# Softmax row sums written to PSUM, one eviction moved from VectorE to ScalarE, three PSUM banks for the rest, and new instruction orders in a fused adaLN block

## The reference

```
mod = silu(c) @ wmod            -> sa, ca, ga, sb, cb, gb per batch
h   = layernorm(x) * (1 + ca) + sa
q, k, v = (h @ W + b).reshape(b, 16 heads, 8, 256)
attn = softmax(einsum('bhdt,bhds->bhts', k, v) * temperature, axis=-1)
x   = x + ga * einsum('bhdt,bhts->bhds', q, attn)
h   = layernorm(x) * (1 + cb) + sb
gate, up = fp4_linear(h, w_gate), fp4_linear(h, w_up)      # 352 wide
x   = x + gb * fp4_linear(silu(gate) * up, w_down)
```

## Time and profile before

| what | value |
|---|---|
| median of three runs | 613.52 us (611.83 to 613.89) |
| the profiled execution's own time | 614.23 us |
| its span, first to last instruction | 611.3 us |
| busy: ACT, DVE, PE, POOL | 555.9, 568.7, 558.3, 507.3 us |
| mean granted TensorE clock | 0.962 |
| one batch in the steady stretch | 17.18 us |

### The profile page before, as it was taken

One profiled execution on the slowest core, in us unless ns is written; L12 is line 12 of the kernel. 1 busy time (PEld: TensorE's weight loads), 2 busy tenths in 40 slices (PEclk: granted clock), 3 DMA queues, 4 the chain that ended last, 5 costly groups with the idle time before them and its releaser, 6 DMA issues.

```text
span 611.3 us, 15522 instructions
## 1 busy us (share of the span) xinstructions
PE 558.3 (91%) x4336; PEld 385.6 (63%) x4336; DVE 568.7 (93%) x1124; ACT 555.9 (91%) x2281; POOL 507.3 (83%) x710
## 2 busy tenths in 40 slices
PE   4588999999999999999999999999999999998874
PEld 2465556666666666666666666666666666666653
DVE  5568799999999999999999999999999999999986
ACT  2499899999999999999999999999999999999621
POOL 5544478999999999999999999999999999988741
PEclk9669899999999999999999999999999999999878
DMA  5655556546655556555655556655655556652000
GB/s 156 179 142 143 129 152 163 145 133 170 170 140 147 149 155 173 159 157 137 172 144 143 149 155 171 171 145 139 170 144 141 152 153 174 164 143 58 10 10 26
DMA packets 87888, 86.12 MB, mean 141 GB/s; under 512 B 8566, under 2 KB 83548, under 8 KB 87804
## 3 DMA queue, kind: packets, MB, share of 16 engines
q1 hardware_dynamic: 85372, 83.10, 50.4%
q10 hardware_dynamic: 2432, 2.03, 1.2%
HBM read 47.29 MB, written 37.81 MB: 139 GB/s over the span
## 4 chain that ended last, share of the span: by engine, by line
ACT 52%; PE 18%; issue 13%; DVE 12%; POOL 3%; ACTq 1%; DVEq 0%; POOLq 0%
ACT probs L825 47%; DVE neg_max L1005 6%; PE score_ps L1502 6%; PE bank L1581 5%; PE bank L1570 3%; ACT hT L835 2%; DVE silu_g L1123 2%; ACT hid_T L859 2%; PE bank L1548 2%; PE bank L1606 1%; ACT q_T L841 1%; DVE h_mag L975 1%; POOL hid_q L367 1%; PE bank L1520 1%; DVE h_mag L979 1%
## 5 line engine op out<-in xcount | busy, mean ns | idle before, releaser
L825 ACT ACTIVATE probs<-score_ps,neg_max 128x256 f32<-128x256 f32 x1024 | 483.5, 552 | 5.4 <-DVE neg_max L1005 4.3
L1005 DVE TENSOR_REDUCE neg_max<-score_ps 128x4 f32<-128x1024 f32 x256 | 312.1, 1219 | 19.5 <-PE score_ps L1502 16.8
L825 ACT ACTIVATION_READ_ACCUMULATOR probs<-score_ps,neg_max 128x1 f32 x1024 | 292.4, 286 | 0.0
L1502 PE MATMUL score_ps<-v_stack,k_stack 128*128 128x256 f32 x1024 | 234.9, 333 | 24.2 <-ACT probs L825 21.7
L1502 PEld LDWEIGHTS score_ps<-v_stack,k_stack 128*128 128x128 f32 x1024 | 156.0, 194 | 108.2 <-ACT probs L825 85.1
L1548 PE MATMUL bank<-probs,q_z 128*32 128x256 f32 x2048 | 132.6, 389 | 0.0
L1548 PEld LDWEIGHTS bank<-probs,q_z 128*32 128x32 f32 x2048 | 57.6, 111 | 42.4 <-issue 3.2
L1606 PEld LDWEIGHTS bank<-wd_T,hid_T 118*128 118x128 f32 x384 | 52.7, 201 | 7.6 <-ACT hid_T L859 1.3
L1606 PE MATMUL bank<-wd_T,hid_T 118*128 118x128 f32 x384 | 56.0, 286 | 0.5 <-ACT hid_T L859 0.5
L1570 PE MATMUL bank<-wgu_T,h_T 128*128 128x352 f32 x128 | 52.0, 488 | 1.7 <-ACT h_T L848 0.5
L367 POOL TENSOR_TENSOR hid_q<-hid_r,hid_sc 128x704 f32<-128x704 bf16 x31 | 43.0, 1387 | 7.6 <-DVE hid_r L362 7.5
(11 more groups left out here) (119 smaller groups left out, 880.9 us busy)
## 6 DMA issues: line engine op xcount, KB each, us to landing
split_dram<-kv_hi SPq DMA_DIRECT2D x124, 128.0 KB, 2.6
split_dram<-kv_lo SPq DMA_DIRECT2D x124, 128.0 KB, 2.6
k_stack<-split_dram SPq DMA_DIRECT2D x124, 128.0 KB, 4.5
v_stack<-split_dram SPq DMA_DIRECT2D x31, 512.0 KB, 4.2
mod_bc<-mod_dram SPq DMA_DIRECT2D x32, 256.0 KB, 4.0
x_in<-in_L_attn_x_dram SPq DMA_DIRECT2D x32, 128.0 KB, 3.1
out_dram<-out_t SPq DMA_DIRECT2D x32, 128.0 KB, 3.6
split_dram<-kv_hi ACTq DMA_DIRECT2D x4, 128.0 KB, 2.4
```

The source lines that it names most:

```text
L825: nc.scalar.activation(probs[p][:, h, a, :], score_ps[:, j % 4, a, :], ACT.Exp, bias=neg_max[:, p, n:n + 1], accum_out=row_sum[:, p, h, a: ...
L1005: nc.vector.tensor_reduce(neg_max[:, p, 4 * u:4 * u + 4], score_ps[:, lo:lo + 2, :, :].rearrange("p b a n -> p (b a) n"), AX.X, ALU.max, n ...
L1502: done = nc.tensor.matmul(score_ps[:, j % 4, a, :], k_stack[p][:, h, 128 * a:128 * a + 128], v_stack[p][:, h // R, :], start=True, stop=True)
```

## The change

The row sums of the exponentials go to a PSUM tensor, `row_ps`, which takes `bank_3`. Once per batch ACT copies them to SBUF (`row_sums_out`, 32 columns), in four quarters for the last batch, and DVE's reciprocal waits for that copy. All other PSUM users share `bank_0` to `bank_2`. The high part of v is made on ACT instead of DVE, and DVE's `k_hi` waits for it, since both read the same bank. The bias matmul of q is gone: q's bias is loaded as a column `b_q` and applied by ACT's eviction. POOL's `normalise2` and `scale2` wait for DVE's exponent and magic number of hid of the batch two back. The orders of all five engines are new; SP stores all four parts of a batch one step later in its own numbering and then loads the stacks.

```diff
-TAIL = 39
+TAIL = 37
-        b_raw = sb("b_raw", [64, 3 * D])
-        b_pad = sb("b_pad", [128, 3 * D], F32R)
-        ones_r = sb("ones_r", [128, T], F32R)
+        b_raw = sb("b_raw", [64, 2 * D])
+        b_q = sb("b_q", [128, 1])
+        b_pad = sb("b_pad", [128, 2 * D], F32R)
+        ones_r = sb("ones_r", [128, 128], F32R)
-        bank_xT, bank_kv, bank_q, bank_h2T, bank_mix, bank_down = bank_1, bank_1, bank_2, bank_0, bank_2, bank_3
-        bank_gate, bank_up, bank_hidT = (bank_2, bank_3), (bank_1, bank_0), (bank_2, bank_0)
-        bank_ffw = (bank_0, bank_3, bank_0)
+        bank_xT, bank_kv, bank_q, bank_h2T, bank_mix, bank_down = bank_0, bank_0, bank_1, bank_2, bank_0, bank_1
+        bank_gate, bank_up, bank_hidT = (bank_2, bank_2), (bank_0, bank_1), (bank_1, bank_2)
+        bank_ffw = (bank_2, bank_2, bank_2)
+        row_ps = bank_3[:, 0:2 * H * 2].rearrange("p (b h a) -> p b h a", b=2, a=2)
...
             def normalise2(b, c):
+                if 2 <= b < NB - 4:
+                    pool.wait_ge(hid_z_made, b - 1)
                 normalise2_on(pool, nc.gpsimd, b, c)
             def scale2(b, c):
+                if 2 <= b < NB - 4:
+                    pool.wait_ge(hid_mag_made, b - 1)
                 scale2_on(pool, nc.gpsimd, b, c)
...
-                                         accum_out=row_sum[:, p, h, a:a + 1]).then_inc(exped, 1)
+                                         accum_out=row_ps[:, p, h, a:a + 1]).then_inc(exped, 1)
+            def row_sums_out(b, c):
+                if b == NB - 1:
+                    return
+                act.wait_ge(exped, 2 * H * (b + 1))
+                wait_batches(act, inv_made, b - 1)
+                nc.scalar.activation(row_sum[:, c % 2, :, :], row_ps[:, c % 2, :, :], ACT.Copy).then_inc(row_sums_made, 1)
+            def row_sums_out_part(b, c, r):
+                act.wait_ge(exped, 2 * H * b + 2 * G * (r + 1))
+                wait_batches(act, inv_made, b - 1)
+                nc.scalar.activation(row_sum[:, c % 2, r:H:R, :], row_ps[:, c % 2, r:H:R, :], ACT.Copy)\
+                    .then_inc(row_part[r], 1)
...
+            def v_hi(b, c):
+                wait_batches(act, kv_ps_made, b + 1)
+                wait_dma(act, split_stored, b - 2, STORES * 16)
+                nc.scalar.activation(halves(kv_hi[c % 2][:, 1, :]), kv_rows(1), ACT.Copy).then_inc(v_hi_made, 1)
             def q_out(b, c):
...
-                nc.scalar.activation(q_T[:, c, :, :], halves(bank_q[:, 0:T]), ACT.Copy).then_inc(qT_made, 1)
+                nc.scalar.activation(q_T[:, c, :, :], halves(bank_q[:, 0:T]), ACT.Identity, bias=b_q[:, 0:1])\
+                    .then_inc(qT_made, 1)
...
             def k_hi(b, c):
-                wait_batches(dve, kv_ps_made, b + 1)
+                wait_batches(dve, v_hi_made, b + 1)
...
-            def v_hi(b, c):
-                wait_batches(dve, kv_ps_made, b + 1)
-                wait_dma(dve, split_stored, b - 2, STORES * 16)
-                nc.vector.tensor_copy(halves(kv_hi[c % 2][:, 1, :]), kv_rows(1)).then_inc(v_hi_made, 1)
...
             def row_sums_inv(b, c):
-                wait_batches(dve, exped, b + 1, 2 * H)
+                wait_batches(dve, row_sums_made, b + 1)
...
-                nc.tensor.matmul(bank_q[:, 0:T], w_q[:, :], hT[:, :], start=True, stop=False)
-                nc.tensor.matmul(bank_q[:, 0:T], b_pad[:, 0:D], ones_r[:, :], start=False, stop=True)\
-                    .then_inc(qT_ps_made, 1)
+                nc.tensor.matmul(bank_q[:, 0:T], w_q[:, :], hT[:, :], start=True, stop=True).then_inc(qT_ps_made, 1)
```

More of the change, by code:

```diff
@@ L913, in _ @@
+            last(row_sums_out_part, 31, 2)
+            last(row_sums_out_part, 31, 3)
+            last(tanh, 29, 1)
             last(hidT_out, 28, 0)
@@ L1265, in step @@
             def step(k):
[L1266 to L1279 removed]
+                at(k, 12, silu, 1)
@@ new lines, in _ @@
+            last(hid_exponent, 25)
+            last(k_hi, 30)
+            last(hid_magic, 25)
+            last(maxes, 28, 7)
+            last(v_lo, 30)
+            last(gate2, 24)
+            last(k_lo, 30)
+            last(maxes, 29, 0)
+            last(silu, 26, 0)
+            last(row_sums_inv, 28)
+            last(maxes, 29, 1)
+            last(times_up, 26, 0)
+            last(maxes, 29, 2)
+            last(silu, 26, 1)
+            last(h2_max, 27)
+            last(maxes, 29, 3)
@@ new lines, in _ @@
+            last(hid_magic, 26)
+            last(gate2, 25)
+            last(k_lo, 31)
+            last(maxes, 30, 0)
+            last(silu, 27, 0)
+            last(row_sums_inv, 29)
+            last(maxes, 30, 1)
+            last(times_up, 27, 0)
+            last(maxes, 30, 2)
+            last(silu, 27, 1)
+            last(h2_max, 28)
+            last(times_up, 27, 1)
+            last(maxes, 30, 3)
+            last(h2_recip, 28)
+            last(maxes, 30, 4)
+            last(h2_exponent, 28)
@@ L1417, in _ @@
             last(hid_exponent, 30)
+            last(residual2, 28)
             last(hid_magic, 30)
+            last(silu, 31, 0)
             last(gate2, 29)
-            last(silu, 31, 0)
+            last(hid_sub, 30)
             last(times_up, 31, 0)
-            last(hid_sub, 30)
             last(silu, 31, 1)
```

798 lines of the change are left out of this document (485 added, 313 removed).

## The result

The changed kernel takes **615.97 us** (median of 11 runs, 615.61 to 618.36) against 611.81 (11 runs, 610.01 to 613.89) for the kernel before on the same chip: ratio 1.0078, 95% interval 1.0061 to 1.0094. It is 0.8% slower, where 599 us was forecast. Its profiled span is 616.3 us against 611.3.

The account below looks back on a forecast made before the run. ACT was taken as the fullest engine, DVE next; after the change DVE would set a batch of 16.65 instead of 17.18 us. 614.2 - 15.9 over 30 batches + 0.5 for the tail gave 599 us, range 590 to 623.

Parts of the forecast that it names:

- the sum: Steady batch: DVE, fullest at 16.61 us, sets 16.65, 0.53 less than 17.18; over 30 batches 15.9 us gained.
- The read's slot: ACT's 32 accumulator reads a batch, now to PSUM: each slot 0.03 us shorter than 0.09, 0.96 us a batch.
- ACT in slots: ACT's work per batch counted from start to next start: 16.79 us before, 17.24 with additions, 16.28 after the reads' saving.
- The first rival: ACT's accumulator read slot does not shrink, so ACT sets the batch: slower, 624 us; 24 in 100.
- 0.39 of 17.18 in which ACT waits unseen: ACT in a batch of the kernel before: 16.79 us of slots leave 0.39 us of hidden waiting.
- the hole of 289.46 to 289.85: ACT before an exponential: slot 0.74 instead of 0.45 us, most of the unseen wait; silu and a maximum on DVE precede.
- Orders and banks: Rewritten orders and three PSUM banks instead of four, at PE: counted at nothing, at worst 0.3 us a batch.
- second and third rivals: Second: partial gain, 607 us, 17 in 100. Third: nothing to be seen, 612 to 615 us, 7 in 100.
- The third: Rival: POOL's wait or the three banks eat all the gain, 612 to 615 us; 7 in 100.
- POOL's new wait: POOL waits for DVE's exponent and magic number: counted at nothing, perhaps 0.3 us a batch if its cover is gone.
- The tail: Last term, at the end: last batch's row sums come through ACT copies, adding 0.5 us (0 to 3).
- The head: Start of the kernel, reordered: counted at 0, within 2 us either way.

Follow-up runs that it names:

- x_sbuf: The changed kernel with the row sums written to SBUF as before, without ScalarE's copies; 3% over the changed kernel, 0.60 us a batch.
- x_vhi_dve: The changed kernel with v's high part back on DVE ahead of k's, without k's wait; same ratio as the changed kernel, batch 0.07 us longer.
- s_dve: The changed kernel with the second silu product cut to 32 of 352 columns in batches 2 to 27 (time only); batch stays 17.14 us.
- b_dve: The kernel before with the second silu product cut to 32 of 352 columns in batches 2 to 27 (time only); nothing gained.
- b_act: The kernel before with the second tanh cut to 32 of 352 columns in batches 2 to 27 (time only); batch 17.20 us, nothing gained.
- x_nopool: The changed kernel without POOL's two waits for DVE's exponent and magic number of hid; 1.6% slower than with the waits.
- b_wait: The kernel before with only POOL's two waits for DVE's exponents and magic numbers added; no difference in time.
- x_headtail: The changed kernel with weight tasks behind the first norm and the last batch's q parts 2 and 3 right behind part 1; tail 38.8 us.
- z_all: The changed kernel with head, tail, k's high part, gate2 and hidT copy moved, last batch first in the tail; 42.1 us behind last accumulator read.

## Why the prediction was wrong

**The step that failed** is in the sum: "The fullest engine is now DVE, 16.61 ... so I take a batch of 16.65. That is 0.53 less than 17.18." Measured, it is 0.05 less; 0.48 x 30 is 14.4 of the 17 us by which the forecast missed. (Head and tail missed by another 7. Against that, the sum was made on an execution 2.4 us above this comparison's median, and the first and last batches gave about 1 us.) Most of the terms under it were not the fault:
- The read's slot: forecast 0.03 shorter, measured 0.04. ACT in slots: forecast 16.28, measured 16.0. The first rival, no saving, is refuted, and x_sbuf shows that the saving is used, 0.60 us a batch.
- v's high part on ACT: forecast 0.27, measured 0.31. The copy of row sums: forecast 0.09, measured 0.08. q's eviction with its bias pointer: forecast 0.27 + 0.09, measured 301.58 - 301.22 = 0.36.
- DVE really lost 0.33. With ACT's 0.3 for it the move gave 0.07 a batch (x_vhi_dve), and s_dve and b_dve took as much again at another place and gained nothing.

What was wrong is the passage from an engine's sum to the batch. The prediction saw "0.39 of 17.18 in which ACT waits unseen" and "they hand a little waiting to each other", and then let that waiting shrink with the work, so that the fullest engine's sum was the batch. DVE was not the bound (s_dve), and ACT's waits grew from 0.39 to 1.1 us a batch while its work shrank by 0.8. They are no slack: the batch goes from engine to engine, and work taken beside that path comes back as a wait, one for one (b_act). The signs were in the rows quoted: PE, DVE and ACT between 97.0 and 99.8% busy, silu, maximum, exponentials taking turns in the chain, and the hole of 289.46 to 289.85, which the prediction found, and followed back to DVE only. The sum of one engine is a lower bound of the batch only.

**Orders and banks** were counted at nothing, "at worst 0.3". (The "0.3 us idle a batch" given for PE there is a slip: its own 17.18 and 16.66 leave 0.52.) They cost, with the smaller parts, 0.56 us a batch (x_sbuf), nearly all of what PSUM gave. That PE waits 0.63 us a batch for k's and v's low parts ahead of up_proj (up to 317.61 in the batch shown) was named as a sign of the second and third rivals, and it is there. The third, "POOL's wait or the three banks eat all of it, 612 to 615", at 7 in 100, is nearest to what happened, though the banks' share is not separated, and POOL's wait is a gain:

**POOL's new wait** was held to cost nothing, perhaps 0.3 a batch. It is worth 10 us in the new orders (x_nopool) and nothing in the old (b_wait). The prediction looked for who waits behind it and not for whom it keeps clear.

**The tail**, "I add 0.5 (0 to 3)", measured 5.0. Its reason, copies through ACT, is minor: they are done by 577.6. What cost is that the last gate comes 7.35 us behind the last accumulator read and not 1.85, in the rewritten order of the last batches on DVE and PE, and that was not walked through; which of the two holds it is open (x_headtail, z_all). "A tail over 3 us longer would be an error of the last term" was right as a test. **The head**, "0, within 2 either way", measured 2.45; the DVE order with a DMA wait ahead of the first norm could be read from the diff.

The range, 590 to 623, held the time, but that was luck: it reached so far for the sake of a rival, the read that does not shrink, that did not come true. The sign, at 69 in 100 for faster, was wrong. Head and tail alone, 7.5 us, would have put even the forecast batch at 606.

## What to carry to other kernels

When several engines are over 95% busy in a hand-ordered pipeline, the batch is set by a path that goes from engine to engine, and no engine's sum gives it. Fold the trace by batch and look at slots, since ends of writes hide waits: where a slot is longer than that of the same instruction elsewhere, the path has left this engine. In these kernels work that the engine did beside such a path was worth nothing, and work in a stretch without holes counted in full. A throwaway kernel that cuts one piece (as b_act) prices the piece at its place, not the engine. Count a rewritten order as a part of the change with its own cost, and walk the first and the last batches through it. A wait can be worth more than it costs, where it keeps one engine out of another's way.

## What the runs showed of the hardware

- ScalarE's accumulator read occupies its engine for 0.05 us with a PSUM target and for 0.09 with an SBUF target, the ACTIVATE ahead of it 0.36 in both (301.66 on, and the earlier trace rows). The Trainium skill (ScalarE: Activation LUTs, Step-by-step: what each stage is for) says that ScalarE reaches PSUM faster than SBUF; the trace agrees for a write of one element per partition, and no run here shows a larger one.
- The ends do not follow the starts: the reads start 0.41 us apart but last 0.16, then 0.18 (307.85, 308.26), and 0.38 at 305.25 after a long run of exponentials, so ends are 0.43 apart. PE may overwrite a score buffer only at the end, so in a long run only a part of the 0.04 us gained per read can reach PE (an estimate: in the kernel before the ends of the reads at 301.29 and 304.43 are seven exponentials and 3.18 us apart, 0.454 each, so 0.02 to 0.03 is left of it).
- A VectorE operation of 0.33 us on bf16 in SBUF (the magic number, 128x704) took 0.73 us when a GpSimd operation on SBUF had started 0.19 us earlier, and ended 0.19 us after it (x_nopool).
- An ACTIVATE's duration is not its cost: the tanh of 352 columns lasts 0.67 us and the next instruction starts 0.42 after it, of which 0.07 is a wait. A tanh of 32 columns lasts 0.43 in b_act, behind a long run of exponentials, and 0.20 at the start of the kernel.
